# The last pass of each projection in two 64-row matmuls, one for each half of the tokens

## The reference

```python
kv_c = x @ W_kvd + b_kvd                       # 64 features for each token
keys_c, values = heads(kv_c @ W_ku + b_ku), heads(kv_c @ W_vu + b_vu)
keys_r = rope(heads(kv_c @ W_kr + b_kr))       # 16 heads of 64
q_c = x @ W_qd + b_qd                          # 192 features for each token
queries_c, queries_r = heads(q_c @ W_qu + b_qu), rope(heads(q_c @ W_qr + b_qr))
scores = concat(queries_c, queries_r) @ concat(keys_c, keys_r).T / sqrt(192)
out = x + softmax(causal(scores)) @ values @ W_o + b_o + ffn(xn)
```

## Time and profile before

| | |
|---|---|
| time of three runs | 1427.53, 1427.95, 1428.28 us (median 1427.95) |
| span of the profiled execution | 1427.6 us |
| PE busy | 1394.7 us (98%), 9786 matmuls |
| PEld busy | 1262.8 us (88%) |
| ACT busy | 1203.2 us (84%) |
| DVE busy | 1151.8 us (81%) |
| POOL busy | 998.3 us (70%) |

### The profile page before, as it was taken

One profiled execution on the slowest core, in us unless ns is written; L12 is line 12 of the kernel. 1 busy time (PEld: TensorE's weight loads), 2 busy tenths in 40 slices (PEclk: granted clock), 3 DMA queues, 4 the chain that ended last, 5 costly groups with the idle time before them and its releaser, 6 DMA issues.

```text
span 1427.6 us, 27603 instructions
## 1 busy us (share of the span) xinstructions
PE 1394.7 (98%) x9786; PEld 1262.8 (88%) x9786; DVE 1151.8 (81%) x2708; ACT 1203.2 (84%) x2603; POOL 998.3 (70%) x573
## 2 busy tenths in 40 slices
PE   6979999999999999999999999999999999999998
PEld 4769999998899999988899999999889999999987
DVE  4858898885788888887678889888677888888888
ACT  4658888997788988898788888899778988888887
POOL 6986777777667877768765777777766777666750
PEclk9999999999999999999999999999999999999999
DMA  9752212212343222211333222221233322221110
GB/s 269 226 126 50 73 50 64 64 49 64 75 106 81 79 64 64 64 44 36 78 93 96 68 68 63 64 64 49 64 75 90 87 58 65 64 63 47 36 27 31
DMA packets 46957, 106.82 MB, mean 75 GB/s; under 512 B 9333, under 2 KB 17830, under 8 KB 46822
## 3 DMA queue, kind: packets, MB, share of 16 engines
q1 hardware_dynamic: 43360, 94.01, 25.7%
q0 software_dynamic: 3296, 11.01, 2.7%
q10 hardware_dynamic: 166, 0.03, 0.0%
HBM read 48.92 MB, written 9.96 MB: 41 GB/s over the span
## 4 chain that ended last, share of the span: by engine, by line
PE 87%; ACT 6%; DVE 2%; SPq 1%; DMA 1%; POOL 1%; issue 1%; POOLq 0%; ACTq 0%; DVEq 0%
PE turn L1554 17%; PE ring L1499 11%; PE u_ps L1575 9%; PE ring L1531 9%; PE ring L1530 9%; PE u_ps L1576 9%; PE ring L1529 8%; PE o_ps L1599 4%; PE o_ps L1600 4%; PE ring L1512 2%; ACT probs L778 2%; PE ring L1438 2%; PE ring L1444 2%; ACT probs_hi L787 1%; DMA swapped<-k_rope 1%; POOL k_rope L367 1%
## 5 line engine op out<-in xcount | busy, mean ns | idle before, releaser
L1076 DVE TENSOR_SCALAR_CACHE_REDUCE probs<-ring,c_t 128x1024 f32<-128x1024 f32 (+7 forms) x512 | 414.3, 810 | 96.6 <-PE ring L1531 92.1
L1086 DVE TENSOR_TENSOR probs_lo<-turn,probs_hi 128x512 fp32r<-128x512 f32 (+1 forms) x640 | 401.2, 630 | 69.0 <-ACT probs_hi L787 64.1
L787 ACT ACTIVATE probs_hi<-turn 128x512 fp32r<-128x512 f32 (+1 forms) x640 | 349.7, 549 | 105.1 <-PE turn L1554 99.3
L778 ACT ACTIVATE probs<-probs,row_min 128x1024 f32<-128x1024 f32 (+7 forms) x512 | 394.3, 771 | 11.8 <-DVE probs L1076 9.2
L1554 PE MATMUL turn<-ident,probs 128*128 128x128 f32 x2304 | 387.2, 275 | 3.2 <-DVE probs_lo L1086 2.3
L1575 PE MATMUL u_ps<-probs_hi,kv_nat 128*128 128x256 f32 x1147 | 312.6, 302 | 1.0 <-DVE u_pair L1092 1.0
L1554 PEld LDWEIGHTS turn<-ident,probs 128*128 128x128 f32 x2304 | 282.9, 140 | 29.0 <-ACT probs L778 6.6
L1576 PE MATMUL u_ps<-probs_lo,kv_nat 128*128 128x256 f32 x1147 | 287.7, 280 | 0.0
L1529 PE MATMUL ring<-k_hi,q_hi 128*128 128x512 f32 (+3 forms) x768 | 275.4, 359 | 0.0
L1531 PE MATMUL ring<-k_hi,q_lo 128*128 128x512 f32 (+3 forms) x768 | 263.1, 343 | 0.0
L1530 PE MATMUL ring<-k_lo,q_hi 128*128 128x512 f32 (+3 forms) x768 | 262.5, 342 | 0.0
(11 more groups left out here) (229 smaller groups left out, 2582.9 us busy)
## 6 DMA issues: line engine op xcount, KB each, us to landing
swapped<-k_rope SPq DMA_DIRECT2D x128, 128.0 KB, 2.3
wv<-wv_scratch SPq DMA_DIRECT2D x62, 256.0 KB, 4.0
wp<-wp_scratch SPq DMA_DIRECT2D x62, 192.0 KB, 3.5
wp<-wp_scratch SPq DMA_DIRECT2D x31, 256.0 KB, 3.1
swapped<-q_y SPq DMA_DIRECT2D x62, 128.0 KB, 2.3
swapped<-q_x SPq DMA_DIRECT2D x62, 128.0 KB, 2.3
k_hi<-qb_kv_hi SPq DMA_DIRECT2D x16, 256.0 KB, 3.7
k_lo<-qb_kv_lo SPq DMA_DIRECT2D x16, 256.0 KB, 4.8
```

Of the source, the lines that this page charges most:

```text
L778: act.activation(p, p, ACT.Exp, scale=-1.0, bias=row_min[:, r:r + 1], accum_out=row_sum[:, g % 4, w, h:h + 1]).then_inc(exp_ready, 1)
L787: act.activation(probs_hi[:, r % 4, 0:width], turn[r % 2][:, 0:width], ACT.Identity).then_inc(turned_hi, 1)
L1076: dve.tensor_scalar(probs_of(g, w, h), ring[slot_of(entry)][:, KEY_COLUMN[qt]:KEY_COLUMN[qt] + keys], c_t[b % 2][:, qt, ds(pair * 2 + h, 1 ...
L1086: dve.tensor_tensor(probs_lo[:, r % 4, 0:width], turn[r % 2][:, 0:width], probs_hi[:, r % 4, 0:width].bitcast(F32), ALU.subtract).then_inc ...
```

## The change

The last pass of each projection is issued with 64 rows in place of 128: only the rows that hold the high part of the features are used, so the product of low weight and low feature is left out of the sum. To let the two halves of the tokens use different rows, the stacks are filled otherwise: for the first 512 tokens the high part lies in rows 0 to 63 and the low part in rows 64 to 127, for the last 512 tokens the other way round. The last pass then takes rows 0 to 63 for the first half of the tokens and rows 64 to 127 for the second. The full passes of both halves come first, then the two 64-row matmuls in a row. The counts of matmuls stay at 4 and 10. The stacks take eight DMAs of 64 rows by 512 tokens for a batch.

```diff
-        ROWS_DMAS, REST_DMAS, ROPE_W_DMAS, STACK_DMAS = 3, 7, 5, 2
+        ROWS_DMAS, REST_DMAS, ROPE_W_DMAS, STACK_DMAS = 3, 7, 5, 4
...
-                    for rows, part in ((slice(0, 64), qb_kv_hi), (slice(64, P), qb_kv_lo)):
-                        sp.dma_start(to[rows, :].bitcast(F32), part[source, :].bitcast(F32)).then_inc(signal, 16)
+                    for c in range(2):
+                        tokens = slice(c * HALF, (c + 1) * HALF)
+                        high_rows, low_rows = slice(c * 64, (c + 1) * 64), slice(64 - c * 64, P - c * 64)
+                        for rows, part in ((high_rows, qb_kv_hi), (low_rows, qb_kv_lo)):
+                            sp.dma_start(to[rows, tokens].bitcast(F32), part[source, tokens].bitcast(F32)).then_inc(signal, 16)
...
+                if k == ROPE_K:
+                    hi, lo = (wp[:, key_column(part):][:, 0:P] for part in range(2))
+                    full, half_weights, half_moving = ((hi, kv_stack),), lo, kv_stack
+                else:
+                    h = k - QUERY_X
+                    (a_hi, b_hi), (a_lo, b_lo) = (
+                        [wp[:, query_column(part, h, rows):][:, 0:P] for rows in range(2)] for part in range(2))
+                    full, half_weights, half_moving = ((a_hi, qa_hi), (a_hi, qa_lo), (a_lo, qa_hi), (b_hi, qb_stack)), b_lo, qb_stack
                 for c in range(2):
                     tokens = slice(c * HALF, (c + 1) * HALF)
-                    if k == ROPE_K:
-                        hi, lo = (wp[:, key_column(part):][:, 0:P] for part in range(2))
-                        passes = ((hi, kv_stack), (lo, kv_stack))
-                    else:
...
-                        passes = ((a_hi, qa_hi), (a_hi, qa_lo), (a_lo, qa_hi), (b_hi, qb_stack), (b_lo, qb_stack))
-                    for n, (w, moving) in enumerate(passes):
-                        mm = pe.matmul(to[:, tokens], w, moving[:, tokens], start=(n == 0), stop=(n == len(passes) - 1))
+                    for n, (w, moving) in enumerate(full):
+                        pe.matmul(to[:, tokens], w, moving[:, tokens], start=(n == 0), stop=False)
+                for c in range(2):
+                    tokens, high_rows = slice(c * HALF, (c + 1) * HALF), slice(c * 64, (c + 1) * 64)
+                    mm = pe.matmul(to[:, tokens], half_weights[high_rows, :], half_moving[high_rows, tokens], start=False, stop=True)
                 mm.then_inc(ring_full, 1)
```

More of the change, by code:

```diff
@@ L1487, in project_pair @@
                         pe.wait_ge(wp_loaded, m * (16 * WP_LOADS))
+                if k == ROPE_K:
[6 more added lines that the diff above has]
+                    full, half_weights, half_moving = ((a_hi, qa_hi), (a_hi, qa_lo), (a_lo, qa_hi), (b_hi, qb_stack)), b_lo, qb_stack
                 for c in range(2):
                     tokens = slice(c * HALF, (c + 1) * HALF)
-                    if k == ROPE_K:
-                        hi, lo = (wp[:, key_column(part):][:, 0:P] for part in range(2))
-                        passes = ((hi, kv_stack), (lo, kv_stack))
-                    else:
-                        h = k - QUERY_X
-                        (a_hi, b_hi), (a_lo, b_lo) = (
-                            [wp[:, query_column(part, h, rows):][:, 0:P] for rows in range(2)] for part in range(2))
-                        passes = ((a_hi, qa_hi), (a_hi, qa_lo), (a_lo, qa_hi), (b_hi, qb_stack), (b_lo, qb_stack))
-                    for n, (w, moving) in enumerate(passes):
-                        mm = pe.matmul(to[:, tokens], w, moving[:, tokens], start=(n == 0), stop=(n == len(passes) - 1))
+                    for n, (w, moving) in enumerate(full):
[3 more added lines that the diff above has]
+                    mm = pe.matmul(to[:, tokens], half_weights[high_rows, :], half_moving[high_rows, tokens], start=False, stop=True)
                 mm.then_inc(ring_full, 1)
```

## The result

The changed kernel takes 1444.51 us (median of 4 runs, 1439.58 to 1445.34) against 1428.12 of the kernel before: a ratio of 1.0106, 95% interval 1.0088 to 1.0123. A second set of runs gave 1441.70 (5 runs, 1441.49 to 1445.54) against 1429.82, ratio 1.0091 (1.0076 to 1.0107). By these ratios it is slower by 13 to 15 us (the medians themselves differ by 16.4 and 11.9). Three of the nine runs, at 1445.3 to 1445.5 us, have a mean granted clock of 0.993 or 0.994, the other six, at 1439.6 to 1443.7, 0.996 to 0.998; two of the three stand in the first set and lift its median.

A forecast was written before the change was run, and what follows sets the result against it. PE, busy 98%, was taken as the bound. 91 projections x 0.25 = 22.8 us, less 1 hidden, plus 2.0 for the stacks, made 23.8 us on the 1427.6 span: about 1451.5 us, range 1425 to 1466.

The forecast's parts named there:

- PE bounds, nothing covers the loss: In the body PE is busy 98%, so about 0.25 us lost per projection lengthens the span almost one for one.
- Overhead of one visit, 0.37: At each projection's 64-row pair, changing from 128 rows and back was to cost 0.14 + 0.17 + 0.06 = 0.37 us.
- way in: Before the 64-row pair, its first load waits until the full matmul is through: 0.14 us.
- middle: Between the 64-row load and the next 128-row load, an exposed load and a second wait for an empty array: 0.17 us.
- way out: Behind the 64-row matmul, the next 128-row load is hidden by nothing: 0.06 us.
- The second load, 0.11: Inside the pair, the second 64-row load can't run ahead and stands 0.11 us behind the first.
- The stacks, 2.0 us: In the first batch, four more stack DMAs at 0.5 us each delay the first swap of rope keys by 2.0 us.
- its own lower edge, 1441: Low end of the forecast's own range, 1441 to 1456 us: second load hidden, 0.14 x 91 + 1.
- the bytes alone set the pace: Lower bound for the first batch's stack DMAs: four more cost nothing, as the bytes stay the same.
- 1 us hidden in ACT's stretches: In ACT's layer-norm stretches, one per batch, up to 2.3 us of loss can hide in PE's free time; 1 us taken off.
- Rival 1: At the projections' change of rows, no wait, and the pair takes one matmul's time: 1409 or 1419 us; chance 0.17.
- 24 us free in ACT: Between 400 and 600 us ACT, the next busiest engine after PE, has 24 us free in 200.

The follow-up runs named there:

- single matmuls: Against the changed kernel, each half's 64-row matmul follows that half's own full passes, so a projection goes to 64 rows twice; 1498.24 us, ratio 1.0480 to before.
- pair on the same rows: Against the changed kernel, stacks as before and both 64-row matmuls on rows 0 to 63; 1461.17 us, ratio 1.0215 to before.

## Why the prediction was right, and where it was off

The time forecast was 1451.5, measured are 1444.5 and 1441.7, 13 to 15 us lost for a forecast of 23.8; the sign, the bound and the mechanism hold, and two terms were too large.

- **PE bounds, nothing covers the loss.** Nearly right: 0.17 is lost at the projection and 0.147 arrives in the step. 30 steps of 0.44 are 13.2 us, and the two traces that start alike differ by 12.7.
- **Overhead of one visit, 0.37.** Right: 0.38 with single matmuls, 0.37 with two one after another, 0.147 + 0.232 = 0.38 with the pair. The split was off by 0.03 to 0.04 each: way in 0.33 - 0.23 = 0.10 for 0.14, middle 0.43 - 0.23 = 0.20 for 0.17, way out 0.22 - 0.12 = 0.10 for 0.06. The 64-row transposes of the earlier trace rows gave the price of another kind of matmul to 0.01 us; as the parts were off in both directions, that closeness is partly luck.
- **The second load, 0.11.** This is the mis-sized term. It was read from two full loads behind each other. In the pair the second load costs nothing: a visit costs 0.38 with one matmul and 0.38 with two on different rows. The two were to start 0.1 apart; together they last 0.50, and one alone lasts 0.49 (1233.09). 91 x 0.11 = 10 us of the forecast are not there, and without them the forecast is its own lower edge, 1441.
- **The stacks, 2.0 us.** Mis-sized by the trace: 0.1 from the first stack DMA to the swap, which came at 41.24 and not 2 us behind 42.16. The runs have 0.7, with an interval from below zero to 2.3. The bound "the bytes alone set the pace" fits the trace.
- **1 us hidden in ACT's stretches.** Right in size: from the third key projection to the last, 29 steps grow by 11.3 and 12.1 us together in the two traces, where 29 x 0.44 is 12.8. So 1.4 and 0.7 are hidden, most of it between the fifteenth and the sixteenth.
- **Rival 1** is wrong on the way in and out and right inside: the pair takes the time of one. The Trainium skill's "TensorE: Matmul & The Clock Gate", Part 3: Packing small matmuls, says that a load for rows that don't collide is pulled ahead of matmuls in flight. The trace agrees inside a pair, where the second load starts 0.01 behind the first (1182.56) while the first matmul runs; behind a full matmul the 64-row load waits (676.76 for 676.43), where a full load runs ahead (676.21). The Trainium skill's "TensorEngine Tiling (Array Packing)", Key Properties, says that a change of the tiling mode drains the engine. The trace agrees: 96 of 96 first loads are held, and the two changes cost 0.38 us.
- The price of rival 1 was wrong too: with PE 0.232 shorter for each projection the time falls by 12.5, not 21, and 3 of that come before the third step; ACT's leaving of `q_x` and DVE's `probs_lo` come next. The earlier trace rows was read as 24 us free in ACT; what counts is when it comes to one evacuation, or to the `u_hi` that DVE waits for. The forecast does not rest on it, as a slower PE moves away from that bound.

No kernel with the whole sum of the change beats before. The one that leaves the last pass out for both halves is the fastest, 1414.35, by doing less.

## What to carry to other kernels

A change between 128 and 64 rows costs a fixed price in both directions together, here 0.38 us, so it pays only if the visit saves more: one pair of 512 columns saves 0.23, and by these numbers it would take two pairs in a visit, 0.46, to come out ahead; no run here has a visit that saves as much. An operation of another kind with the same change in the trace of before gives that price; a second cost put on top of it (the load of a neighbour) should be asked for its own row. Before a gain on the bounding engine is multiplied out, leave the work out once and see what the time does: here less than half of the first 0.70 us saved in a step arrived.

## What the runs showed of the hardware that was not expected

Weight loads of 64 rows on different rows do not queue for each other: their starts are 0.00 to 0.01 us apart, where two loads on the same rows stand 0.11 apart (0.29 for two with 0.18 for one, pair on the same rows). Pairs of matmuls follow each other every 0.23 us with both halves at work. And two traces of one kernel differ by 1.8 us in the first 117 us, with the granted clock at 0.53 from 72 to 83 us in one and at 0.54 from 92 to 99 us in the other; that the clock makes the difference was not tried by itself.
